# A feed-forward layer moved into the block of the attention layer ahead of it

## What is computed

```python
x = x + _L0_xattn_ref(_layernorm(x), ctx_1024, ctx_1024)      # 16 heads
x = x + _L0_ffn_ref(_layernorm(x), ...)                       # 8 experts, top 2
x = x + _L1_xattn_ref(ctx_1024, _layernorm(x), ...)           # 16 heads, with projections
x = x + _L1_ffn_ref(_layernorm(x), ...)
```

```python
h = jax.nn.relu(jnp.einsum('bsd,hd->bsh', x, w1) + b1)        # 256 -> 1024
hq = float_quantize(h, 4, 3)                                  # FP8
out = jnp.einsum('bsh,dh->bsd', hq, wq) + bq                  # 1024 -> 256
out = float_quantize(out, 5, 10)                              # half precision
```

## Time and profile before

| | |
|---|---|
| runs | 1306.88, 1303.41, 1314.79 us; median 1306.88 |
| the profiled execution | 1303.23 us, of which the span (first to last instruction) 1301.5 us |
| mean granted TensorE clock | 0.954 |
| busy share of PE, PEld, DVE, ACT, POOL | 88%, 75%, 70%, 57%, 45% |

### The profile page before, as it was taken

The page is one execution under the profiler, slowest core; times in us unless marked ns, Lnnn a source line. Parts: engine busy times, 40 slices in busy tenths (PEclk is TensorE's granted clock), DMA queues, the critical chain, the costliest instruction groups (busy, mean ns, idle before and its releaser), DMA issues. The chain is left out here.

```text
span 1301.5 us, 28241 instructions
## 1 busy us (share of the span) xinstructions
PE 1149.7 (88%) x10239; PEld 970.1 (75%) x10240; DVE 915.4 (70%) x1261; ACT 740.0 (57%) x978; POOL 580.2 (45%) x555
## 2 busy tenths in 40 slices
PE   3788998969789999999999999547899999949998
PEld 2455665658789999999999999535666666637887
DVE  7898998739268777878778777477888888523432
ACT  3476777856355555554564555315777777724443
POOL 1476676443368686832011000257777774001221
PEclk9999999979989999999999999866999999979999
DMA  5656756438854556443131110256666654211221
GB/s 186 211 196 222 241 202 211 138 119 308 302 170 147 169 174 220 135 140 105 48 113 40 40 48 33 78 186 211 204 212 203 203 206 175 65 54 33 66 64 65
DMA packets 120984, 193.43 MB, mean 149 GB/s; under 512 B 12160, under 2 KB 64384, under 8 KB 120768
## 3 DMA queue, kind: packets, MB, share of 16 engines
q1 hardware_dynamic: 95840, 140.71, 32.0%
q0 software_dynamic: 12576, 39.07, 9.7%
q10 hardware_dynamic: 12480, 12.47, 2.9%
HBM read 91.80 MB, written 49.55 MB: 109 GB/s over the span
## 5 line engine op out<-in xcount | busy, mean ns | idle before, releaser
L1866 ACT ACTIVATE hidden<-hidden 128x1024 f32<-128x1024 f32 x78 | 82.8, 1061 | 186.2 <-DVE hidden L1899 175.3
L1813 PE MATMUL h_ps<-slot_xT_hi,tile_w_hi 128*128 128x256 f32 x624 | 178.0, 285 | 3.0 <-DVE slot_xT_lo L1917 3.0
L1829 PE MATMUL y_ps<-e_w_hi,hiddenT_hi 128*128 x624 | 179.7, 288 | 0.3 <-DVE hiddenT_lo L1923 0.3
L1813 PE MATMUL h_ps<-slot_xT_lo,tile_w_hi 128*128 128x256 f32 x624 | 177.7, 285 | 0.0
L1813 PE MATMUL h_ps<-slot_xT_hi,tile_w_lo 128*128 128x256 f32 x624 | 177.6, 285 | 0.0
L1829 PE MATMUL y_ps<-e_w_hi,hiddenT_lo 128*128 x624 | 176.6, 283 | 0.0
L1829 PE MATMUL y_ps<-e_w_lo,hiddenT_hi 128*128 x624 | 176.5, 283 | 0.0
L1179 DVE TENSOR_REDUCE neg_max<-big 128x4 fp32r<-128x1024 f32 x128 | 155.3, 1221 | 29.8 <-PE big L967 26.8
L602 DVE TENSOR_REDUCE neg_max<-big 128x4 fp32r<-128x1024 f32 x128 | 155.2, 1222 | 18.7 <-PE big L403 16.2
L534 ACT ACTIVATE probs<-big 128x1024 f32<-128x1024 f32 x128 | 131.1, 1024 | 56.2 <-PE big L414 55.3
L1107 ACT ACTIVATE probs<-big 128x1024 f32<-128x1024 f32 x128 | 131.1, 1026 | 43.0 <-PE big L978 38.2
(11 more groups left out here) (232 smaller groups left out, 2700.8 us busy)
## 6 DMA issues: line engine op xcount, KB each, us to landing
k_stack<-k_cut SPq DMA_DIRECT2D x96, 256.0 KB, 2.5
q_stack<-q_cut SPq DMA_DIRECT2D x96, 256.0 KB, 3.0
slots_out<-slot_y ACTq DMA_DIRECT2D x39, 256.0 KB
slots_in<-staging POOLq DMA_DIRECT2D x38, 256.0 KB
slot_x<-slots_in SPq DMA_DIRECT2D x38, 256.0 KB
vals<-in_v_wide SPq DMA_DIRECT2D x16, 512.0 KB, 4.4
v_wide<-v_out SPq DMA_DIRECT2D x16, 512.0 KB, 5.9
vals<-v_wide SPq DMA_DIRECT2D x16, 512.0 KB
```

The source lines that it names most:

```text
L1813: last = nc.tensor.matmul(h_ps[k][:, f % HF, :], w1[w][b.u][:, c, f * P:(f + 1) * P], xT[a][b.u][:, c, :], start=(n == 0), stop=(n == 3 * ...
L1829: last = nc.tensor.matmul(y_ps[o.u][:, q, :], hT[a][o.u][:, f, q * P:(q + 1) * P], of_place(expert_w["w2"][w], f, place), start=(n == 0), ...
L1866: nc.scalar.activation(half(hidden, k), half(hidden, k), ACT.Gelu).then_inc(gelu_done, 1)
```

## The change

The function `feed_forward` and its block are gone. The layer is now a class, `FeedForward`, with one method for each piece of work, and it is made within `second_attention`, on views of that function's tiles (there is no new large tile and no barrier between the layers). x is on the tiles `rows`, the normalized rows on `probs[0]`, the output on `probs[1]` and `[2]`, the FP8 tile on `probs[3]` and `[4]`, the half-precision output on `probs[5]`, the turned halves on `k_cut` and `q_cut`, the bias on `k_in[0]`; in PSUM the turned rows are on one `big` tile, the up-projections on a second, the down-projections on the third and on the two `spare` tiles.

Chunk 0 is started inside the attention's steps: its load behind step 14 on SP, its norm at g = 5 of step 15 on VectorE, its turn at g = 2 of step 16, and four of its eight up-projections at g = 5 and g = 7 of step 16. Behind step 17 the rest follows as before, from up-projection 4 of chunk 0. Chunk 1's x is also loaded behind step 14. The instructions of chunks 1 to 7 are the same in number, size and order.

```diff
+EARLY_UP = 4
...
+class FeedForward:
...
+    def tensor(self, pe):
+
+        def body(b):
+            n = b.shift(1)
+            if self.has(b.t):
+                for f in range(EARLY_UP if b.t0 == 0 else 0, FC):
+                    self.up(pe, b, f)
+            if self.has(n.t):
+                self.turn(pe, n)
+            if self.has(b.t):
+                for q in range(self.CT):
+                    self.down(pe, b, q)
+        self.run(pe, body, 0)
...
         @block.sync
...
             for b in range(FIRST, END):
                 body(b)
+                if b == BATCHES - 2:
+                    sp.wait_ge(k_cut_step, 2 * (BATCHES - 1))
+                    ffn.load_b2(sp)
+                    sp.wait_ge(x2_step, BATCHES * TOP)
+                    for chunk in (chunk0, chunk1):
+                        for u in range(2):
+                            sp.wait_ge(stored[u], (chunk.t + 1) * 16)
+                        ffn.load_x(sp, chunk)
             for u in range(2):
                 sp.wait_ge(stored[u], BATCHES // 2 * 16)
+            ffn.sync(sp)
...
         @block.tensor
...
                     elif g == 2:
                         if has(b + 3):
                             project_q(b + 3)
+                        if b == BATCHES:
+                            last_of_big(pe, turn_bank)
+                            ffn.turn(pe, chunk0)
...
                     elif g == 5:
                         if has(b):
                             pv(b, 1)
+                        if b == BATCHES:
+                            last_of_big(pe, up_bank)
+                            pe.wait_ge(up_lo, len(UP_BATCHES))
+                            for f in range(EARLY_UP // 2):
+                                ffn.up(pe, chunk0, f)
...
                     elif g == 7:
                         if has(b):
                             pv(b, 2)
+                        if b == BATCHES:
+                            for f in range(EARLY_UP // 2, EARLY_UP):
+                                ffn.up(pe, chunk0, f)
 
             for b in range(FIRST, END):
                 body(b)
+            last_of_big(pe, rows_bank)
+            for s in range(2):
+                last_of_spare(pe, s)
+            ffn.tensor(pe)
...
         @block.scalar
...
                     elif g == 2:
                         if has(b + 3):
                             q_hi_out(b + 3)
+                        if b == BATCHES:
+                            for u in range(2):
+                                act.wait_ge(k_stacked[u], BATCHES // 2 * PARTS)
+                                act.wait_ge(q_stacked[u], BATCHES // 2 * PARTS)
+                            for c in range(KC):
+                                ffn.hi(act, chunk0, c)
                     elif g in (3, 5, 7):
                         if has(b):
                             pv_out(b, (g - 3) // 2)
+                        if b == BATCHES and g > 3:
+                            for f in range(EARLY_UP // 2):
+                                ffn.relu(act, chunk0, f + (g - 5) // 2 * (EARLY_UP // 2))
...
         @block.vector
...
                     elif g == 2:
+                        if b == BATCHES:
+                            for c in range(KC):
+                                ffn.lo(dve, chunk0, c)
...
+                    elif g == 5:
+                        if b == BATCHES - 1:
+                            ffn.convert_b2(dve)
+                            full_spare(dve, (("pv", 0), b))
+                            ffn.norm(dve, chunk0)
...
-def feed_forward(nc, const, dram, weights):
...
         second_attention(nc, const, dram, weights)
-        if phases < 5:
-            return
-        feed_forward(nc, const, dram, weights)
```

More of the change, by code:

```diff
@@ L790, in read_big, with as_one, halves, last_of_big @@
             eng.wait_ge(big_freed[bank], turn + 1)
+        def as_one(t, dt, n, m):
+            flat = t[:].rearrange({3: "p a b -> p (a b)", 4: "p a b c -> p (a b c)"}[len(t.shape)])
+            return (flat if dt is None else flat.bitcast(dt)).rearrange("p (m n) -> p m n", n=n)[:, 0:m, :]
+        by_end = sorted(range(3), key=lambda bank: max(n for use, (at, n) in bigs.at.items() if at == bank and use[0] != "out"))
+        rows_bank = bigs.place(("out", BATCHES - 1))[0]
+        turn_bank, up_bank = [bank for bank in by_end if bank != rows_bank]
+        CT, CHUNK = FeedForward.CT, FeedForward.CHUNK
+        def halves(bank):
+            return [big[bank][:, par].rearrange("p q s -> p (q s)") for par in range(2)]
+        out16 = as_one(probs[5], F16, DIM, 2 * CT)
+        ffn = FeedForward(ctx, nc, const, dram, weights, {
+            "x": [as_one(rows[u], None, DIM, CT) for u in range(2)], "normed": as_one(probs[0], None, DIM, CT),
+            "out": [as_one(probs[1 + u], None, DIM, CT) for u in range(2)],
+            "h8": [as_one(probs[3 + u], FP8, CHUNK, FC) for u in range(2)], "out16": [out16[:, u * CT:(u + 1) * CT, :] for u in range(2)],
+            "xT": [[as_one(k_cut[0], None, CHUNK, KC), as_one(q_cut[0], None, CHUNK, KC)],
+                   [as_one(k_cut[1], None, CHUNK, KC), as_one(q_cut[1], None, CHUNK, KC)]],
+            "b2": k_in[0][:, 0, :], "b2_16": k_in[0][:, 1, 0:DIM // 2].bitcast(F16),
+            "xT_ps": halves(turn_bank), "h_ps": halves(up_bank), "y_ps": halves(rows_bank) + [spare[s][:] for s in range(2)],
+        })
+        chunk0, chunk1 = static_step(0), static_step(1)
+        def last_of_big(eng, bank):
+            eng.wait_ge(big_freed[bank], sum(at == bank for at, n in bigs.at.values()))
+        def last_of_spare(eng, bank):
+            eng.wait_ge(freed[bank], sum(at == bank for at, n in spares.at.values()))
         block = ctx.enter_context(nc.Block())
@@ L954, in _ @@
             pool.wait_ge(up_lo, len(UP_BATCHES))
+            ffn.gpsimd(pool)
         @block.tensor
@@ L1168, in _ @@
                 body(b)
+            ffn.scalar(act)
         @block.vector
@@ L1277, in _ @@
                 body(b)
+            ffn.vector(dve)
 def constants(nc, const):
```

304 lines of the change are left out of this document (144 added, 160 removed).

## The result

| | median | runs |
|---|---|---|
| before | 1305.14 us | 1302.13 to 1314.79, 4 runs |
| after | 1289.33 us | 1288.82 to 1290.77, 4 runs |

The ratio is 0.9888, 95% interval 0.9852 to 0.9925: 14.6 us less, between 10 and 19. The profiled execution of after took 1290.77 us (span 1289.0, clock 0.961), 12.5 us less than that of before.

The account below looks back on a forecast made before the run. The layer's start was taken as bound by latency, not an engine. 18.2 us less at full clock minus 1.5 for the clock gives 16.7, 1286.5 from the profiled 1303.23; put a little higher at 1288, range 1282 to 1297.

Parts of the forecast that it names:

- The total: Whole kernel: 18.2 us less at full clock, minus 1.5 for the clock, 16.7 us less; forecast 1288 us.
- The seam: From project_out(14) to up-projection 4 of chunk 0: 18.2 us shorter at full clock, 16.7 with the clock's fall.
- attT_lo late: Step 15, VectorE: chunk 0's norm ahead of batch 14's attT_lo delays project_out(14), costing 2.6 us on the path.
- halves' gap: Step 16: from the end of chunk 0's turn to its first up-projection, 1.99 us for the high and low halves.
- the new wait for `spare`: Ahead of up-projection 4: TensorE waits for add_out(15), since down-projections use the two spare tiles; 1 us.
- the clock: Near project_out(14): the new 3.0 us hole drops TensorE to 1.2 GHz for some 3 us, costing 1.5 us.
- The rule of the Trainium skill: Rival B, no fall: only single long pauses lower the clock, so 18.2 us less, 1286 us; chance 0.19.
- the row of the kernel before: Between 1149.0 and 1152.6 TensorE is busy 1.22 of 3.60 us, pauses at most 1.47; then granted clock 0.50.
- Loads: Chunk 0's x, loaded behind step 14, lands by 1136, VectorE asks at 1141.9: 6 us of cover, no cost.
- chunk 1's norm: Behind add_out(15) on VectorE: ends at 1166.3, TensorE wants it at 1167.2; fits with 0.9 us to spare.
- pace of the chunks: Chunks 2 to 7 keep the same producers and order; 15.3 us from chunk to chunk.
- Behind it, the same instructions follow in both kernels, so the difference of these stretches is the difference of the kernels: Behind up-projection 4 of chunk 0: nothing differs, so the gain in the 34.91 us stretch ahead is the whole gain.

Follow-up runs that it names:

- a0: The changed kernel (after) run again unmodified beside the variants on the same chip: 1290.88 us, ratio to before 0.9893.
- e1: after plus one more GpSimd drain behind the last weight split of the attention's steps: 1288.04 us, ratio to before 0.9883.
- e2: e1 plus one more indirect DMA of 128 rows behind the early drain, into a tile nothing reads: 1288.76 us, one execution.
- e5: after without early up-projections; chunk 0's eight up-projections all stand behind step 17: 1291.63 us, ratio to before 0.9917.
- e6: after with the waits for the third large and both small tiles ahead of the first down-projection, not up-projection 4: 1287.8 us, 0.9900 of before.
- e9: after plus one more GpSimd drain behind step 9, right behind the last of its 64 gathers: 1293.05 us, one execution.
- e10: after plus one more GpSimd drain behind step 5, so that 16 of the 64 gathers come behind it: 1289.76 us, one execution.
- e3: after with chunk 0's cast and norm behind batch 14's attT_lo instead of ahead of it: 1284.59 us, ratio to before 0.9857.
- e4: after with chunk 0's cast and statistics at g = 2 of step 15, only the normalizations at g = 5: 1283.19 us, 0.9857 of before.
- e8: after with three edits together: early drain (e1), split norm (e4), later tile waits (e6): 1280.92 us, ratio to before 0.9825.
- e11: e8 with chunk 0's turn and halves moved to g = 7 of step 15, behind pv(15, 2): 1280.59 us, ratio to before 0.9819.
- e7: after with only the loads early; chunk 0's norm, turn, halves and all ups behind step 17: 1293.79 us, ratio to before 0.9949.

## Why the prediction was right, and what it missed

- **The total.** 16.7 us was forecast; the ratio gives 14.6, and the traces from the common zero to the last instruction 165.08 - 150.84 = 14.2. 1288 was forecast and 1289.33 measured, in the range. That they are so close is partly luck. Counted from the profiled execution of before, the forecast was 1286.5, and that of after took 1290.77: 4.3 more, of which 2.2 are the drain, which the forecast left out, and 1.8 were lost ahead of the common zero, where nothing was changed. The 1.5 us that were added for the scatter of the executions, and a median that lies 1.4 below that execution, made up for most of it.
- **The seam.** Up-projection 4 came 43.64 - 27.22 = 16.4 us earlier, against 16.7. Term by term: attT_lo late by 2.5 (2.6), halves' gap as before, the new wait for `spare` 1.06 (1 us), the clock 1.55 (1.5).
- **The clock.** The fall came where it was put, for about as long. It came in all eight profiled executions with this hole (2.83 to 2.91 us: after, a0, e1, e2, e5, e6, e9, e10), and in the four that have a wait of 1.35 us or less there (e3, e4, e8, e11) the clock stayed at 1.00. The rule of the Trainium skill (TensorE: Matmul & The Clock Gate, section HAM oscillation), under which it should have stayed, speaks of longer pauses than the 2.91 us here; the trace does not agree. But the row of the kernel before, on which the forecast rested, is no sure guide either: e7 has its three waits of 0.77, 1.18 and 1.47 us, and the clock stayed at 1.00 behind them. So the forecast of the fall was right on a ground that need not have held, which is luck in part. Why the clock fell behind these waits once and once not, the runs leave open.
- **Loads, chunk 1's norm, pace of the chunks.** Each as forecast: no wait for the load, none ahead of chunk 1's turn, 112.6 and 112.7 us from up-projection 4 to the last.
- **The step that failed** is "Behind it, the same instructions follow in both kernels, so the difference of these stretches is the difference of the kernels". The tensor work is the same, but the end of the block is not: GpSimd's drain of 64 gathers moved from a place where it was hidden to the end, and gave back 2.2 us. The row was in the trace of before: 5.3 us at 1111.1, 42 us ahead of its use, and I had looked at timelines that leave sequencer instructions out. e1 shows that this is the cause: with the drain moved off the end, the last instruction comes 2.4 us earlier.
- **The two parts of the gain.** The interleaving was worth 7.6 us and the removed barrier, store and load 8.5 (at up-projection 0). The forecast had not separated them, and in the expectation of e7 I put 11 and 7.7.

## What to carry to other kernels

When two blocks are made one, list what stood in the barrier of the first: each engine's drain moves to the next barrier, and what was hidden in mid-kernel may end it. Work that is moved ahead into a latency-bound stretch should be cut so that its pieces go into the idle time of their own engine; ahead of an instruction that another engine waits for, it costs what of it goes beyond the idle time that was there (here 2.5 of its 4.9 us) and perhaps the clock (here 1.5). A wait for a tile belongs directly ahead of its first writer, not at the head of the phase.

## What the runs showed of the hardware

- GpSimd's drain at the end of the attention block took 0.787 us with no indirect DMA since the last drain, 0.862 with one (e2), 2.087 with 16 (e10) and 6.012 with 64 (after): about 0.08 us for each of these gathers. The last sum of 0.67 us is within each of the four. The drain of the experts' block, with 74 other indirect DMAs and 47 plain ones since the last drain, was through 1.0 us behind the vector work (before), so the price is not one for every indirect DMA.
- A drain behind the last gathers took 9.0 us in mid-work (e9) and 5.3 where GpSimd was idle (e1), so it should be put there.
- TensorE, idle for 2.83 to 2.91 us between dense stretches, was granted 1.2 GHz in place of 2.4 in the next stretch, in eight executions of eight; idle for 1.35 us (e3), it kept 2.4. Behind waits of 0.77, 1.18 and 1.47 us with short work between, it was granted 1.2 GHz in one execution (before) and kept 2.4 in another (e7).
